# Attention scores lowered by their row maximum before the transpose, the exponential taken on the way out of PSUM

## The chip, the cores and the metric

The kernel runs on one core of a Trainium2 chip. The metric is the device time of one execution in microseconds (us); lower is better.

## The reference

One transformer block on x of 8 x 512 tokens x 256 features, all in float32. Attention comes first, then a mixture of experts:

```python
h = layernorm(x) * (1 + ca) + sa
q, k, v = split(h @ W_qkv + b_qkv)                      # 16 heads of 16
scores = q @ k.T / 4 + bias[h, i - j]                   # 512 x 512 for each of 8 x 16 heads
attn = softmax(scores, axis=-1)
x = x + ga * ((attn @ v) @ W_out + b_out)
h = layernorm(x) * (1 + cb) + sb
x = x + gb * (layernorm(sum of the 2 best of 8 experts) + h)
```

An expert is w_down(gelu(w_up(h))) with 1024 inner units. The change lies in the softmax of the attention alone.

## The kernel before, in words

The kernel has four stages: `prepare` (layer norm, the gates), `attention`, `route` (which token goes to which expert) and `experts`. Each engine runs a program of its own, written out by hand in the order in which it shall be done, and semaphores hold them together. There is no planner.

In `attention`, an outer loop runs over the 8 batches and an inner one over the 16 heads n (0 to 15) of a batch. The inner loop is written out. Batch 0 ("first") and batch 7 ("last") are written out too, and batches 1 to 6 ("middle") are one loop of the program (`Fori` in `by_batches`, L402), which every engine turns for itself. A head's scores are a 512 x 512 matrix, in four tiles t of 128 rows x 512 columns. For each head the engines do this:

- TensorE (`score`, L883) multiplies a tile of queries by the keys into one of two banks `ps_s`. The bank of tile t is free when VectorE has read tile t - 2 (`biased`).
- VectorE (`add_bias`, L753) adds the bias from the table `s_tile`, writes the negated sum into `sn` and takes its minimum over the row, the negated row maximum, into `mn`. It waits until the exponential has read that tile of `sn` for the head before (`exped`).
- ScalarE (`exp`, L680) writes exp(mn - sn) into `pr`, one tile of 128x512 at a time, four a head.
- TensorE (`turn_probabilities`, L891) transposes the 16 blocks of 128x128 of `pr` into the four banks `ps_t`, in two halves ("pairs") of eight.
- VectorE (`evacuate`, L764) copies the first half of `ps_t` (128x1024) into `pt`, ScalarE (`evacuate`, L685) the second half.
- TensorE (`weigh`, L900) multiplies `v`, which has a column of ones for the row sums, by `pt` into `ps_o`.

The heads overlap: in its stretch for head n TensorE does the scores of n, the transposes of n - 1 and the weighing of n - 2. The order is L1001 to L1017: scores 0 and 1, the shared use of n, transposes (first half), score 2, transposes (second half), score 3, weighing of n - 2. The shared uses (`USES`, L306) are the small works of the batch before and after, all through one bank `ps_m`: the projections q0, k0, q1, k1, v0, v1 of the next batch (at heads 1, 2, 9, 10, 12, 13), the transposes of results back0 to back3, turn0, turn1, rows0, rows1, the output projections out0 and out1 (heads 6 and 8), and the gate's logits (15.5, that is after head 15). ScalarE and VectorE read `ps_m` in the same order and free it (`used`, `freed`).

VectorE also has `moments` (after head 9), `centre` (L814, after head 10) and `normal` (L822, after head 12), of the batch before. GpSimd has work beside the heads, in an order of its own (`batch`, L631): it splits queries and keys into three bf16 parts (`split`, L409), splits a quarter of an expert's weights into two (`split_piece`, L571), adds the residual (`residual`, `add_x`), does `deviation` and `rest_of` for the layer norm, and moves v into place (`move_v`, L563). SP (`batch`, L504) issues the DMAs: loads of x and of weight pieces, stores of the parts and pieces after `split_done` and `w_low`, and reloads of the parts as stacks `qs` and `ks` for the next batch after head 7 and after head 15.

## Time and profile before

| | us |
|---|---|
| median of 3 runs | 1393.21 (1391.31 to 1395.48) |
| the profiled execution | 1397.81 |
| its span | 1396.2 |
| TensorE busy | 1152.0 (83%) |
| VectorE busy | 927.5 (66%) |
| ScalarE busy | 676.1 (48%) |
| GpSimd busy | 709.6 (51%) |
| the exponential, L683, ScalarE | 340.8, 512 instructions |
| the add of the bias, L761, VectorE | 332.3, 512 instructions |
| the transposes, L897, TensorE | 280.3, 2048 matmuls |
| the copy of the first half, L769, VectorE | 156.4, 128 instructions |
| the copy of the second half, L690, ScalarE | 131.2, 128 instructions |

The profile names engines PE (TensorE; PEld is its weight load), DVE (VectorE), ACT (ScalarE), POOL (GpSimd) and SP (the DMA issuer). In a row of the timeline stand start, duration, engine, line, operation, tile written and tiles read, shapes, count, and in brackets the idle time before it and who ended it. Matmuls are pipelined: a row's duration runs to the end of the last one, and the next can begin before it. A span of the profile is some 1.6 us less than the execution's own time.

### The profile page before, as it was taken

To read this page: it belongs to the slowest core of one execution; us is meant where nothing else is said; L and a number is where in the kernel's file an instruction comes from. 1 tells how busy PE (TensorE), PEld (TensorE's weight loads), DVE (VectorE), ACT (ScalarE), POOL (GpSimd) and SP (SyncE) were. 2 spreads that over 40 slices of the span, in tenths; PEclk is the share of its full clock that TensorE was granted. 3 is DMA by queue.
4 is the path that set the end of the run, shared out by engine and by line. 5 is a ranking of instruction groups with operands and counts; after the bars stand their busy time and mean duration, and the time that the engine had idled before them with its cause. 6 is when DMAs were issued, how large, how long until landed. Compare 5 with 4: busy or idle time off the path is not lost. (4 is left out here: it accounts for less than half of the span.)

```text
span 1396.2 us, 33418 instructions
## 1 busy us (share of the span) xinstructions
PE 1152.0 (83%) x11298; PEld 900.9 (65%) x11299; DVE 927.5 (66%) x2197; ACT 676.1 (48%) x1044; POOL 709.6 (51%) x726
## 2 busy tenths in 40 slices
PE   5569999898998998988999861399999999999900
PEld 3236776676766765766677541188888888888800
DVE  4548788587786885885888836655555555555566
ACT  4247776575765765765677620222222222222312
POOL 3215155343551553454423322866776777676756
PEclk9779999898998998998999975599999999999955
DMA  9597952663556346526644117124243344242364
GB/s 308 180 194 193 255 158 79 150 129 99 152 111 156 110 101 144 123 84 144 120 98 142 61 46 268 34 48 106 45 105 80 72 111 108 50 106 45 45 159 127
DMA packets 123679, 169.23 MB, mean 121 GB/s; under 512 B 13176, under 2 KB 99704, under 8 KB 123552
## 3 DMA queue, kind: packets, MB, share of 16 engines
q1 hardware_dynamic: 103136, 137.59, 37.3%
q0 software_dynamic: 20416, 29.94, 11.2%
q8 instruction: 80, 1.31, 0.4%
q14 instruction: 47, 0.39, 0.1%
HBM read 106.26 MB, written 61.23 MB: 120 GB/s over the span
## 5 line engine op out<-in xcount | busy, mean ns | idle before, releaser
L683 ACT ACTIVATE b_pr<-b_sn,b_mn 128x512 f32<-128x512 f32 x512 | 340.8, 714 | 133.1 <-DVE b_mn L761 128.8
L761 DVE CUSTOM_DVE_ANT_0 b_sn<-b_ps_s,s_tile 128x512 f32<-128x512 f32 x512 | 332.3, 685 | 91.0 <-PE b_ps_s L888 36.1
L897 PE MATMUL b_ps_t<-b_ident,b_pr 128*128 128x128 f32 x2048 | 280.3, 282 | 8.5 <-ACT b_pr L683 7.4
L897 PEld LDWEIGHTS b_ps_t<-b_ident,b_pr 128*128 128x128 f32 x2048 | 246.0, 146 | 54.2 <-ACT b_pr L683 21.2
L888 PE MATMUL b_ps_s<-b_ks,b_qs 96*128 96x512 bf16 x512 | 195.2, 403 | 58.7 <-DVE b_mn L761 31.6
L1594 PE MATMUL d_ps_u<-d_xp,k_wu 128*128 128x256 bf16 x1776 | 201.6, 274 | 0.0
L1609 PE MATMUL d_ps_y<-k_wd,d_gp 128*128 128x256 bf16 x1776 | 199.9, 273 | 0.0
L769 DVE COPY b_pt<-b_ps_t 128x1024 f32<-128x1024 f32 x128 | 156.4, 1222 | 54.9 <-PE b_ps_t L897 50.9
L1594 PEld LDWEIGHTS d_ps_u<-d_xp,k_wu 128*128 128x128 bf16 x1776 | 173.6, 98 | 21.7 <-issue 0.8
L1609 PEld LDWEIGHTS d_ps_y<-k_wd,d_gp 128*128 128x128 bf16 x1776 | 173.7, 98 | 20.2
L690 ACT ACTIVATE b_pt<-b_ps_t 128x1024 f32<-128x1024 f32 x128 | 131.2, 1025 | 108.5 <-PE b_ps_t L897 107.9
L1484 ACT ACTIVATE d_g<-d_ps_u 128x512 f32<-128x512 f32 x160 | 94.8, 598 | 129.4 <-PE d_ps_u L1594 128.9
L1437 POOL DMA_INDIRECT sums<-d_yo,d_places x80 | 133.2, 1665 | 41.6 <-issue 24.9
L912 PE MATMUL b_ps_o<-b_pt,b_v 128*32 128x128 f32 x4096 | 144.6, 284 | 0.2 <-ACT b_pt L690 0.2
L1520 DVE CAST d_xp<-d_ps_x 128x512 bf16<-128x512 f32 x41 | 28.3, 691 | 169.3 <-PE d_ps_x L1581 169.3
L912 PEld LDWEIGHTS b_ps_o<-b_pt,b_v 128*32 128x32 f32 x4096 | 108.3, 113 | 43.9 <-issue 42.6
L1493 ACT ACTIVATE d_yo<-d_ps_y,d_gates 128x256 f32<-128x256 f32 x80 | 33.5, 470 | 198.6 <-PE d_ps_y L1609 176.4
L888 PEld LDWEIGHTS b_ps_s<-b_ks,b_qs 96*128 96x128 bf16 x512 | 49.2, 98 | 114.9 <-DVE b_mn L761 71.8
L1533 DVE TENSOR_TENSOR d_gp<-d_g,d_gp 128x512 bf16<-128x512 f32 x160 | 110.8, 693 | 5.5
L1414 POOL DMA_INDIRECT d_xg<-h_rows,d_tokens x84 | 88.2, 1050 | 49.4 <-POOL d_tokens L1410 36.4
L1426 POOL DMA_INDIRECT d_gates<-gate_rows,d_places x80 | 77.2, 965 | 44.4 <-POOL d_places L1422 31.7
L1531 DVE CAST d_gp<-d_g 128x512 bf16<-128x512 f32 x160 | 74.4, 465 | 35.6 <-ACT d_g L1484 29.8
(192 smaller groups left out, 1244.7 us busy)
## 6 DMA issues: line engine op xcount, KB each, us to landing
w_parts<-b_w_split SPq DMA_DIRECT2D x32, 512.0 KB, 3.4
splits<-b_parts SPq DMA_DIRECT2D x32, 384.0 KB, 2.6
b_qs<-splits SPq DMA_DIRECT2D x96, 128.0 KB, 4.9
b_ks<-splits SPq DMA_DIRECT2D x96, 128.0 KB, 7.2
b_w_raw<-in_w_up_t SPq DMA_DIRECT2D x16, 512.0 KB, 8.9
b_w_raw<-in_w_down_t SPq DMA_DIRECT2D x16, 512.0 KB, 5.7
k_wu<-w_parts SPq DMA_DIRECT2D x8, 1024.0 KB, 4.9
k_wd<-w_parts SPq DMA_DIRECT2D x8, 1024.0 KB, 7.3
```

The lines of the kernel that those rows point to most:

```text
L683: act.activation(pr[:, m, t, :], sn[:, t, :], ACT.Exp, bias=mn[:, m, t:t + 1], scale=-1.0).then_inc(exped, 1)
L690: act.activation(pt[:, m, 2:4, :], ps_t[:, 2:4, :], ACT.Copy).then_inc(out_act, 1)
L761: dve.tensor_tensor_reduce(sn[:, t, :], ps_s[:, t % 2, :], ahead.tile[:, n, at:at + S], -1.0, BIG, ALU.add, ALU.min, mn[:, n % 2, t:t + 1] ...
L769: dve.tensor_copy(pt[:, m, 0:2, :], ps_t[:, 0:2, :]).then_inc(out_dve, 1)
L888: pe.matmul(ps_s[:, t % 2, :], qs[:, half, m, t * P:(t + 1) * P], ks[:, half, m, :], start=True, stop=True).then_inc(scored, 1)
L897: mm = pe.transpose(ps_t[:, j, t * P:(t + 1) * P], pr[:, m, t, j * P:(j + 1) * P], ident[:, :])
L912: mm = pe.matmul(ps_o[2 * DK * t:2 * DK * (t + 1), n % TB * P:(n % TB + 1) * P], v[:, j, n, :], pt[:, n % 2, j, t * P:(t + 1) * P], start= ...
L1437: pool.indirect_dma_start(sums, bass.IndirectOffsetOnAxis(ap=places[:, u, 0, i:i + 1], axis=0), yo[:, u, i, :], None, compute_op=ALU.add). ...
L1484: act.activation(g[:, j, :], ps_u[:, j, :], ACT.Gelu).then_inc(gelued, 1)
L1533: dve.tensor_tensor(gp[:, u, 1, at], g[:, j, :], gp[:, u, 0, at], ALU.subtract).then_inc(g_split, 1)
L1594: mm = pe.matmul(ps_u[:, j // 2, j % 2 * ROWS:(j % 2 + 1) * ROWS], kept.wu[:, slot, w, c, j * P:(j + 1) * P], xp[:, u, x, c * ROWS:(c + 1) ...
L1609: mm = pe.matmul(ps_y[:, i, 0:D], gp[:, u, x, j * ROWS + i * P:j * ROWS + (i + 1) * P], kept.wd[:, slot, w, j, :], start=(j == 0 and n == ...
```

## The change

The negated biased scores of a head now stay in `sn` as two buffers (one for even and one for odd heads), and `pr` is gone. Taking the maximum off is a step of its own, in place: GpSimd does tiles 0, 1 and 2 of a head (`lower`: multiply by -1, add the column of `mn`), ScalarE tile 3. TensorE transposes these lowered scores (`turn_scores`). ScalarE alone reads `ps_t`, both halves of 128x1024, and its exponential writes `pt`. VectorE has no evacuation left.

In TensorE's order the weighing of n - 2 comes behind scores 0 and 1 of head n, then the shared use, score 2, the first half of the transposes, score 3, the second half. VectorE's add waits for the transposes of the head before the last (`turned`).

GpSimd's side work is cut into pieces and placed between its `lower`s (`beside`, by head and half head): `split` becomes `split_high` and `split_low`, `split_piece` becomes `piece_high` and `piece_low`, and `residual` and `rest_of` are done in halves, the residual's add as two instructions of 128x512 in place of four of 128x256. The places are: move_v(1) at 0.5; splits 0 and 1 at heads 2 and 3, each high part before the first `lower` and low part between the second and third; residual at 4; pieces 0 and 1 at 5 and 6; add_x at 7 and 9; splits 2 and 3 at 10 and 11; deviation at 11.5; pieces 2 and 3 at 12 and 13; rest_of at 14 and 14.5; move_v(0) at 15.

```diff
@@ -338,9 +338,8 @@
         ks = sb("ks", [KS, 2, HALF, S], BF16)
         v_next = sb("v_next", [P, TB, D])
         v = sb("v", [P, TB, NH, 2 * DK])
-        sn = sb("sn", [P, TB, S])
+        sn = sb("sn", [P, 2, TB, S])
         mn = sb("mn", [P, 2, TB])
-        pr = sb("pr", [P, 2, TB, S])
         pt = sb("pt", [P, 2, TB, S])
         ot = sb("ot", [P, S])
         inv = sb("inv", [P, TB, TB])
...
+            def split_high(k, done, reads):
+
+                pool.wait_ge(freed, reads)
+                at_least(pool, parts_out[k % 2], (done - k % 2) * 8)
+                apart(pool, pool_passed)
+                pool.tensor_copy(parts[:, k % 2, 0, :], qf[:, k % 2, :]).then_inc(split_step, 1)
+                pool.wait_ge(split_step, done * 3 + 1)
+                pool.tensor_tensor(rest[:, :], qf[:, k % 2, :], parts[:, k % 2, 0, :], ALU.subtract).then_inc(split_step, 1)
+
+            def split_low(k, done):
+
+                pool.wait_ge(split_step, done * 3 + 2)
+                apart(pool, pool_passed)
+                pool.tensor_copy(parts[:, k % 2, 1, :], rest[:, :]).then_inc(split_step, 1)
+                pool.wait_ge(split_step, done * 3 + 3)
+                pool.tensor_tensor(parts[:, k % 2, 2, :], rest[:, :], parts[:, k % 2, 1, :], ALU.subtract).then_inc(split_done, 1)
+
...
+            def lower(b, n, t):
+
+                k = (b * NH + n) * TB + t
+                pool.wait_ge(biased, k + 1)
+                apart(pool, pool_passed)
+                pool.tensor_scalar(sn[:, n % 2, t, :], sn[:, n % 2, t, :], -1.0, mn[:, n % 2, t:t + 1], ALU.mult, ALU.add
+                                   ).then_inc(lower_pool, 1)
...
+            def beside(b, n, kind):
+
+                first, last = kind == "first", kind == "last"
+                if n == 0 and kind == "middle":
+                    load_h1(b + 1, uses_before(b, kind) - 1)
+                if n == 0.5 and not first:
+                    move_v(b, 1, uses_before(b, kind) - 1)
+                if n == 2 and not last:
+                    split_high(0, (b + 1) * 4, use(b, kind, "q0") + 1)
+                if n == 2.5 and not last:
+                    split_low(0, (b + 1) * 4)
...
+                for n in range(NH):
+                    beside(b, n, kind)
+                    lower(b, n, 0)
+                    lower(b, n, 1)
+                    beside(b, n + 0.5, kind)
+                    lower(b, n, 2)
...
@@ -677,17 +739,19 @@
                                ACT.Identity, bias=b_col[:, c:c + 1],
                                scale=(DK ** -0.5 if name[0] == "q" else 1.0)).then_inc(freed, 1)
 
-            def exp(h, m, t):
-
-                act.wait_ge(biased, h * TB + t + 1)
-                act.activation(pr[:, m, t, :], sn[:, t, :], ACT.Exp, bias=mn[:, m, t:t + 1], scale=-1.0).then_inc(exped, 1)
-
-            def evacuate(h, m):
-
-                act.wait_ge(turned, h * 2 + 2)
+            def lower(b, n):
+
+                t = TB - 1
+                act.wait_ge(biased, (b * NH + n) * TB + t + 1)
+                act.activation(sn[:, n % 2, t, :], sn[:, n % 2, t, :], ACT.Identity, bias=mn[:, n % 2, t:t + 1], scale=-1.0
+                               ).then_inc(lower_act, 1)
+
+            def exp(h, m, pair):
+
+                act.wait_ge(turned, h * 2 + pair + 1)
 
                 at_least(act, weighed, h - 1)
-                act.activation(pt[:, m, 2:4, :], ps_t[:, 2:4, :], ACT.Copy).then_inc(out_act, 1)
+                act.activation(pt[:, m, 2 * pair:2 * pair + 2, :], ps_t[:, 2 * pair:2 * pair + 2, :], ACT.Exp).then_inc(exped, 1)
 
             def turn_out(c, at):
 
...
@@ -715,14 +779,11 @@
                 for n in range(NH):
                     h = b * NH + n
 
-                    at_least(act, turned, (h - 1) * 2)
-                    exp(h, n % 2, 0)
-                    exp(h, n % 2, 1)
                     read_shared(b, n, kind)
                     if kind != "first" or n > 0:
-                        evacuate(h - 1, (n + 1) % 2)
-                    exp(h, n % 2, 2)
-                    exp(h, n % 2, 3)
+                        exp(h - 1, (n + 1) % 2, 0)
+                        exp(h - 1, (n + 1) % 2, 1)
+                    lower(b, n)
                     if n == 1 and kind != "first":
 
                         outputs(b * GROUPS - 1, uses_before(b, kind))
...
@@ -755,18 +817,11 @@
                 k = (b * NH + n) * TB + t
                 dve.wait_ge(scored, k + 1)
 
-                at_least(dve, exped, k - TB + 1)
+                at_least(dve, turned, (b * NH + n - 1) * 2)
                 apart(dve, dve_passed)
                 at = (TB - 1 - t) * P
-                dve.tensor_tensor_reduce(sn[:, t, :], ps_s[:, t % 2, :], ahead.tile[:, n, at:at + S], -1.0, BIG, ALU.add, ALU.min,
+                dve.tensor_tensor_reduce(sn[:, n % 2, t, :], ps_s[:, t % 2, :], ahead.tile[:, n, at:at + S], -1.0, BIG, ALU.add, ALU.min,
                                          mn[:, n % 2, t:t + 1]).then_inc(biased, 1)
-
-            def evacuate(h, m):
-
-                dve.wait_ge(turned, h * 2 + 1)
-
-                at_least(dve, weighed, h - 1)
-                dve.tensor_copy(pt[:, m, 0:2, :], ps_t[:, 0:2, :]).then_inc(out_dve, 1)
 
...
-            def turn_probabilities(h, m, pair):
-
-
-                at_least(pe, out_act if pair else out_dve, h)
-                for j in (2 * pair, 2 * pair + 1):
-                    for t in range(TB):
-                        mm = pe.transpose(ps_t[:, j, t * P:(t + 1) * P], pr[:, m, t, j * P:(j + 1) * P], ident[:, :])
+            def turn_scores(h, m, pair):
+
+
+                at_least(pe, exped, (h - 1) * 2 + pair + 1)
+                for t in range(TB):
+                    if pair == 0:
+                        if t < TB - 1:
+                            pe.wait_ge(lower_pool, h * (TB - 1) + t + 1)
+                        else:
+                            pe.wait_ge(lower_act, h + 1)
+                    for j in (2 * pair, 2 * pair + 1):
+                        mm = pe.transpose(ps_t[:, j, t * P:(t + 1) * P], sn[:, m, t, j * P:(j + 1) * P], ident[:, :])
                 mm.then_inc(turned, 1)
 
             def weigh(b, n):
 
                 h = b * NH + n
-                pe.wait_ge(out_dve, h + 1)
-                pe.wait_ge(out_act, h + 1)
+                pe.wait_ge(exped, h * 2 + 2)
...
                         pe.wait_ge(stack_in[n // HALF], (b + 1) * 32 * len(Q_PART))
                     score(b, n, 0)
                     score(b, n, 1)
-                    shared(b, n, kind)
-                    if kind != "first" or n > 0:
-
-                        pe.wait_ge(exped, h * TB)
-                        turn_probabilities(h - 1, (n + 1) % 2, 0)
-                        score(b, n, 2)
-                        turn_probabilities(h - 1, (n + 1) % 2, 1)
-                    else:
-                        score(b, n, 2)
-                    score(b, n, 3)
                     if n > 1:
                         weigh(b, n - 2)
                     elif kind != "first":
                         weigh(b - 1, n + NH - 2)
+                    shared(b, n, kind)
+                    score(b, n, 2)
+                    if kind != "first" or n > 0:
+                        turn_scores(h - 1, (n + 1) % 2, 0)
+                    score(b, n, 3)
+                    if kind != "first" or n > 0:
+                        turn_scores(h - 1, (n + 1) % 2, 1)
                     shared(b, n + 0.5, kind)
 
             by_batches(pe, batch)
-            pe.wait_ge(exped, B * NH * TB)
             for pair in range(2):
-                turn_probabilities(B * NH - 1, 1, pair)
+                turn_scores(B * NH - 1, 1, pair)
             weigh(B - 1, NH - 2)
             weigh(B - 1, NH - 1)
             back(B * GROUPS - 1, end_use("back3"))
```

## Rows read from the trace of the kernel before

**Rows 1.** Windows, core 0: busy us (instructions) by engine, TensorE's clock, DMA share, GB/s

```profile
core 0: us, PE busy (x) PEld busy (x) DVE busy (x) ACT busy (x) POOL busy (x), PEclk, DMA share, GB/s
...
264.94:359.68 94.74, 87.47 (x929) 64.76 (x928) 71.76 (x174) 63.48 (x92) 41.43 (x40) 0.93 0.53 122
...
90.00:825.00 735.00, 671.41 (x7347) 498.11 (x7346) 562.85 (x1352) 500.22 (x723) 305.72 (x292) 0.95 0.53 130
```

**Rows 2.** Timeline of ScalarE: L690 at head 1 of batches, and the last

```profile
90.95 1.02 ACT L690 ACTIVATE b_pt<-b_ps_t 128x1024 f32<-128x1024 f32 x1 [1.78 <-PE b_ps_t L897]
...
169.69 1.02 ACT L690 ACTIVATE b_pt<-b_ps_t 128x1024 f32<-128x1024 f32 x1 [1.19 <-PE b_ps_t L897]
...
645.81 1.03 ACT L690 ACTIVATE b_pt<-b_ps_t 128x1024 f32<-128x1024 f32 x1 [1.19 <-PE b_ps_t L897]
...
731.75 1.02 ACT L690 ACTIVATE b_pt<-b_ps_t 128x1024 f32<-128x1024 f32 x1 [0.78 <-PE b_ps_t L897]
...
810.78 1.02 ACT L690 ACTIVATE b_pt<-b_ps_t 128x1024 f32<-128x1024 f32 x1 [2.67 <-PE b_ps_t L897]
```

**Rows 3.** Timeline of one head of batch 5, 566.4 to 571.2 us

```profile
566.46 1.32 ACT L683 ACTIVATE b_pr<-b_sn,b_mn 128x512 f32<-128x512 f32 x2
...
566.66 0.67 PE L888 MATMUL b_ps_s<-b_ks,b_qs 96*128 96x512 bf16 x2
...
567.17 0.60 PE L943 MATMUL b_ps_m<-b_flip,b_on 128*128 128x128 f32 x4
...
567.84 1.09 PE L897 MATMUL b_ps_t<-b_ident,b_pr 128*128 128x128 f32 x8
...
568.77 0.38 PE L888 MATMUL b_ps_s<-b_ks,b_qs 96*128 96x512 bf16 x1
...
568.99 1.04 PE L897 MATMUL b_ps_t<-b_ident,b_pr 128*128 128x128 f32 x8
...
570.06 1.02 ACT L690 ACTIVATE b_pt<-b_ps_t 128x1024 f32<-128x1024 f32 x1 [0.18 <-PE b_ps_t L897]
...
570.17 1.08 PE L912 MATMUL b_ps_o<-b_pt,b_v 128*32 128x128 f32 x32
...
571.18 0.39 PE L888 MATMUL b_ps_s<-b_ks,b_qs 96*128 96x512 bf16 x1
```

**Rows 4.** Timeline, the turn of the loop from batch 1 to batch 2

```profile
245.96 1.02 ACT L690 ACTIVATE b_pt<-b_ps_t 128x1024 f32<-128x1024 f32 x1 [1.10 <-PE b_ps_t L897]
...
249.18 0.19 DVE L833 COPY logits<-b_ps_m 128x32 f32 x1 [1.88 <-PE b_ps_m L966]
...
253.26 1.92 PE L897 MATMUL b_ps_t<-b_ident,b_pr 128*128 128x128 f32 x8
...
255.84 0.69 DVE L761 CUSTOM_DVE_ANT_0 b_sn<-b_ps_s,s_tile 128x512 f32<-128x512 f32 x1 [6.46 <-issue]
...
264.94 1.02 ACT L690 ACTIVATE b_pt<-b_ps_t 128x1024 f32<-128x1024 f32 x1 [1.02 <-PE b_ps_t L897]
```

**Rows 5.** Timeline of TensorE, a head with a projection, batch 0

```profile
92.58 1.88 PE L929 MATMUL b_ps_m<-s_h,s_wqkv 128*128 128x512 f32 x4
94.30 0.93 PE L897 MATMUL b_ps_t<-b_ident,b_pr 128*128 128x128 f32 x7
```

**Rows 6.** By source line, L568, L618, L1175 (from 890.8 us), L819, L828: ns min/median/max

```profile
L568 POOL COPY b_v<-b_v_next x16: 604/609/620, 71.2 to 747.6; 128x512 f32<-128x512 f32 x16
...
L618 POOL TENSOR_SCALAR b_rstd<-b_mv x8: 227/228/496, 214.0 to 831.0; 128x4 f32<-128x4 f32 x8
...
L1175 POOL TENSOR_SCALAR c_hot_rest<-c_nums,c_place_f x7: 595/597/614, 890.8 to 894.3; 128x128 bf16<-128x128 f32 x7
...
L819 DVE SCALAR_TENSOR_TENSOR b_xb<-b_gated,b_mv,b_mod x32: 472/826/2335, 217.5 to 832.1; 128x256 f32<-128x256 f32 x32
...
L828 DVE SCALAR_TENSOR_TENSOR b_xb<-b_xb,b_rstd,b_mod x32: 473/478/484, 231.6 to 834.1; 128x256 f32<-128x256 f32 x32
```

**Rows 7.** Groups of GpSimd's instructions, 264.94 to 359.68 us

```profile
L419 POOL TENSOR_TENSOR b_rest<-b_qf,b_parts 128x512 f32<-128x512 f32 x4 | 4.7, 1174 | 0.3
```

More of the change, by code:

```diff
@@ L407, in by_batches, with split @@
             batch(B - 1, "last")
-        def split(engine, k, done, reads, passed=None):
+        def split(engine, k, done, reads):
             engine.wait_ge(freed, reads)
@@ L414, in split @@
             out = parts[:, k % 2, :, :]
-            if passed is not None:
-                apart(engine, passed)
             engine.tensor_copy(out[:, 0, :], qf[:, k % 2, :]).then_inc(split_step, 1)
@@ L659, in _ @@
+            def batch(b, kind):
+                for n in range(NH):
[4 more added lines that the diff above has]
+                    lower(b, n, 2)
             by_batches(pool, batch)
-            residual(B - 1)
+            for j in range(2):
+                residual(B - 1, j)
             for j in range(2):
@@ L663, in _ @@
             deviation(B - 1)
-            rest_of(B - 1)
+            for j in range(2):
+                rest_of(B - 1, j)
         @block.scalar
@@ L737, in _ @@
             by_batches(act, batch)
-            evacuate(B * NH - 1, 1)
+            for pair in range(2):
+                exp(B * NH - 1, 1, pair)
             outputs(B * GROUPS - 1, uses_before(B - 1, "last") + len(uses_of("last")))
@@ L871, in _ @@
             by_batches(dve, batch)
-            evacuate(B * NH - 1, 1)
             back(B - 1, 3, end_use("back3"))
```

119 lines of the change are left out of this document (68 added, 51 removed).

## The prediction, made before the change was run

> **What bounds the kernel now.** I read the windows first. The attention stage runs from about 90 to 825 us, 735 of the 1396 us, and TensorE is busy for 671 of them [rows 1]; every line that the change touches is in this stage, so the rest of the kernel is taken as unchanged. Next came ScalarE's timeline. One instruction, the evacuation at L690, occurs once a head, so its starts mark the heads: the 16 heads of batch 0 take 78.7 us, batches 1 to 5 take 95.2 us each (476.1 for five), batch 6 takes 85.9 and the 15 heads left take 79.0 [rows 2]. Then one head in the timeline [rows 3]. From its first score matmul (566.66) to the next head's (571.18) there are 4.52 us, and TensorE works nearly all through: two scores to 567.17, a shared use of 0.6 us, eight transposes every 0.93 us (567.84 to 568.77), 0.22 us for a score (568.77 to 568.99), 1.18 for the second eight and the last score, 1.01 for the weighing (570.17 to 571.18). Its waits are short. The reader should see why: every instruction waits for something of an earlier half head. The weighing in particular uses a head whose evacuation ended long before. Without the 0.6 us the work is 0.51 + 0.93 + 0.22 + 1.18 + 1.01 = 3.85 us a head. Last, the turn of the loop [rows 4]: VectorE stands 6.5 us with the releaser "issue" (249.4 to 255.8), and so it goes at the end of each of batches 1 to 5; heads 0 and 1 together take 19.0 us there (245.96 to 264.94). The change keeps the loop, so it keeps this stall.
>
> **What the change moves.** VectorE loses a copy of 128x1024 (1.22 us a head) and ScalarE has two PSUM exponentials of 128x1024 and one pass of 128x512 in place of four exponentials and a copy, 2.8 us a head for 3.9. Both were already under the 4.5 us of a head, so this gains only where they stop TensorE: heads 2 to 15 take 95.2 - 19.0 = 76.2 us, and TensorE's own work in them is 14 x 3.85 + 16.8 for shared uses (below) = 70.7, so there are 5.5 us a batch to be had, some of them where VectorE does moments and centre (L806 to L820) between two adds. TensorE has the same matmuls. What decides is their order and their waits.
>
> **The ring.** Before, the exponential came ahead of the transposes, and weighing head n-2 stood at the end of head n. Now the exponential comes behind the transposes, and weighing n-2 stands behind the first two scores of head n. But the second half of the transposes of n-2 is the last thing in head n-1. So only two scores (about 0.5 us) lie between the transposes and a weighing that waits for the exponential of their result. Everything else of TensorE lies behind that weighing, in the same order, and leads to the next head's transposes. It is a closed ring:
> - from the start of the second eight transposes to ScalarE's start on them: 570.06 - 568.99 = 1.07;
> - the exponential of 128x1024 from PSUM: no row has it; the copy of the same tile and size takes 1.02 to 1.03, taken as 1.03 (lower end: the same, as the engine reads and writes the same elements; two exponentials of 128x512 take 1.32, the upper end);
> - ScalarE's end to TensorE's start: 566.46 + 1.32 = 567.78, and the transposes behind it begin at 567.84: 0.05;
> - weighing 1.01, a score 0.22, eight transposes 0.93, a score 0.22.
> All from [rows 3]. The sum is 4.53 us a head plus any shared use, because shared uses stand inside the ring. TensorE idles about 0.7 us in each head. A head with no shared use took about 4.5 before and stays so; one with a 0.6 us use went for the same 4.5 and becomes 5.1; one with a projection (1.72 us, 92.58 to 94.30 [rows 5]) took 5.6 and becomes 6.25.
>
> **The sum.** Batches 1 to 5, heads 2 to 15: 14 x 4.53 = 63.4; five projections 8.6; two output projections, of about 1.7, 3.4; seven uses of 0.6, 4.2 (the eighth, 0.6 more of work, is at 14.5 and stands in the idle 0.7); and 1.5 for VectorE's centre at head 11: four instructions of 0.83 us at the median [rows 6] ahead of that head's first add, of which the ring's own wait covers about half; the ends are 0 and 4. That is 81.1. At the turn of the loop two things change: the logits no longer stand behind a score and a weighing, so VectorE's stall begins 1.3 us sooner; and eight transposes, which were done inside the stall (253.26, 1.92 us at half clock [rows 4]), now come after it, behind the third score. I take 20.3 for heads 0 and 1, which took 19.0. Batch: 101.4 against 95.2, +6.2, five times +31. Batch 6 without the stall: 81.1 + 5.7 + 4.5 = 91.4 against 85.9, +5.5. Batch 0: 16 x 4.53 + 6 x 1.72 + 3 x 0.6 = 84.6 against 78.7, +5.9. Batch 7: 68.0 for its heads, 3.4, 4.2, 2 at head 11 and 1.2 for the logits, 78.8 against 79.0: nothing. The last head's exponential before the last weighing: +1. Together +43.
>
> **GpSimd.** It gets 48 passes of 128x512 f32 a batch, each with a column from memory and two operations. No row has this form. Below stands the copy of that size, 0.61; above, a line through the two TENSOR_SCALARs of the trace, 0.228 for 4 columns and 0.597 for 128 with little beside it, which is 3.0 ns a column and 1.74 us for 512 [rows 6]. I take 0.70: like the copy it reads and writes one f32 tile, while the 128 columns belong to a comparison that writes bf16. The whole side work of a batch was 41.4 us busy [rows 1]; with 48 x 0.70 = 34 and some 0.1 us between 88 instructions it is 84 of 101, room on the whole. Locally it isn't even: a head with a split is 2 x 0.61 + 2 x 1.17 [rows 7] + 2.1 + 0.7 for gaps = 6.4 us against 5.1 at head 3. The third pass of a head is ready about 1.1 us after its third score and wanted a head later, so some 4 us of lag are covered; the splits and pieces of heads 2 to 6 use 2 to 3 of it. Heads 11 to 14 (two splits, pieces, two products of 128x512) touch the limit: 0.5 a batch, +4. SP's stores wait for the same splits as before, each now due half a batch or more before its stack is loaded; nothing there is near.
> The 128x512 pass is the one cost on which a page speaks with a figure. The Trainium skill's "GPSIMD Engine Reference" (section on elementwise, side-by-side cycle accounting) gives 769 ns for 512 elements in a good loop; the sum would then be higher by about 3 us, and no run so far has this form.
> The trace also shows an interference: the centre's instruction (two SBUF inputs) takes 472 to 2335 ns [rows 6], while its twin L828, for which GpSimd mostly stands idle, takes 473 to 484. With GpSimd busier, all four could take 2.3, 9.3 us instead of four medians, 3.3: at most +6 in each of seven batches, +42; I take none of it, since VectorE has room there. The Trainium skill's "SBUF — State Buffer" (who interferes with whom) says that such a VectorE instruction contends with a GpSimd one that reads SBUF; the trace agrees, and by that rule the scores' add (one input from PSUM) would stay at its 0.68 us.
>
> **Time.** +43 +4 = +47. The profiled execution took 1397.8 us (span 1396.2), 4.6 over the median of the runs, so 1445 becomes 1440 us against 1393.2.
>
> **Rivals.**
> - *TensorE is bound by its work alone.* If the weighing found its exponential done, a head would cost 3.85 plus uses, and VectorE's lost copy would also remove its stops: heads 2 to 15 would take 70.7 + 1.5 = 72.2 where they took 76.2. That is -4 a batch, some -30: 1363. It decides if ScalarE's exponential ended within the 0.5 us of the two scores; 1.07 + 1.03 from the row speak against it. Chance 0.07.
> - *GpSimd is the bound.* Beyond 101 = 48 X + 41 + 9, X = 1.07 us, every head waits for it. At 1.07 its crowded heads exceed the cover by about 9 a batch: near 1515. At 1.74 a middle batch takes 134, the first and last some 117: 1040 for the 720 of now, near 1700. For it: two operations with a pointer may be slower than a copy. Against: the rows of one input. Chance 0.15.
> - *The losses and gains cancel*, if the ring is 0.35 us shorter than its sum (a faster exponential, transposes let go by parts): within 0.3%, 4 us, about what a measurement of this kernel can tell from no change. Chance 0.03.
> The forecast has 0.75. Its own bounds: the ring 0.15 shorter and no stop at head 11, -29: 1411; an exponential of 1.34 adds 0.31 to each of 128 heads, +40, or the interference +42, 1482; GpSimd up to 1.07, 1515. The range 1408 to 1515 leaves out most of the 0.10 below and about half of the second rival. Slower 0.90, within 0.03, faster 0.07.
>
> **What would show it.** Right: TensorE's weighing is preceded by an idle of about 0.7 us released by ScalarE's exponential in nearly every head; ScalarE's second exponential repeats every 4.5, 5.1 or 6.3 us; batches of about 101 us; GpSimd's pass near 0.7 us, and few waits of the transposes for it. Wrong: weighings that start right behind the scores; passes over 1 us with the transposes waiting for GpSimd; a stop at the loop's turn that grew by more than 2 us; times outside attention that moved.

## The result, and the profile of the changed kernel

The changed kernel takes 1480.85 us (median of 4 runs, 1476.11 to 1486.82) against 1394.35 us (4 runs, 1391.31 to 1401.67) before: ratio 1.0625, interval 1.0581 to 1.067. It is slower by 86 us. The profiled execution has a span of 1474.5 us, 78.3 more than the 1396.2 of before.

The page of the changed kernel: the busy time of each engine, and of its part 5 (line, engine, operation, tiles, shapes, count; busy us, mean ns; idle us before them and what ended most of it) the groups of the change:

```profile
PE 1151.9 (78%) x11298; PEld 897.2 (61%) x11299; DVE 796.4 (54%) x2069; ACT 562.2 (38%) x788; POOL 963.5 (65%) x1094
...
L823 DVE CUSTOM_DVE_ANT_0 b_sn<-b_ps_s,s_tile 128x512 f32<-128x512 f32 x512 | 341.3, 689 | 280.2 <-PE b_ps_s L940 275.3
L643 POOL TENSOR_SCALAR b_sn<-b_sn,b_mn 128x512 f32<-128x512 f32 x384 | 264.0, 695 | 194.8 <-DVE b_mn L823 194.1
L754 ACT ACTIVATE b_pt<-b_ps_t 128x1024 f32<-128x1024 f32 x256 | 262.1, 1024 | 298.7 <-PE b_ps_t L954 290.6
...
L968 PE MATMUL b_ps_o<-b_pt,b_v 128*32 128x128 f32 x4096 | 145.7, 285 | 101.1 <-ACT b_ot L765 53.9
```

TensorE is busy for as long as before (1152.0), VectorE for 131 us less, ScalarE for 114 less, GpSimd for 254 more. GpSimd's new pass costs 0.695 us, and the PSUM exponential of 128x1024 costs 1.024. GpSimd's idle before its pass ended with VectorE's maximum (194.1 of 194.8 us), so it was early and not late. TensorE's weighing stood idle for 101 us.

The attention stage shows where the time is. Windows of the changed kernel, a middle batch and the stage (to be read beside [rows 1]; 90 to 902 us answers to 90 to 825 there):

```profile
283.98:388.08 104.10, 85.72 (x929) 63.09 (x928) 56.23 (x158) 49.52 (x60) 72.78 (x86) 0.97 0.49 115
90.00:902.00 812.00, 668.50 (x7338) 494.83 (x7338) 433.52 (x1222) 389.91 (x471) 553.97 (x655) 0.96 0.47 118
```

TensorE's busy time in the stage (668.5 for 671.4) and its clock (0.96 for 0.95) are as before; the stage is 77 us longer. All of the loss is TensorE standing idle in this stage. By the starts of the first exponential of each head, batch 0 takes 92.4 us, batches 1 to 5 take 102.6, 104.1, 110.3, 104.7 and 106.9, batch 6 takes 96.2, and the 15 heads left 82.3: 799.5, where [rows 2] give 719.8.

Two heads of the changed kernel's timeline, to be read beside [rows 3]. The first exponential shown belongs to a head with a 0.6 us use:

```profile
620.33 2.12 ACT L754 ACTIVATE b_pt<-b_ps_t 128x1024 f32<-128x1024 f32 x2 [0.50 <-PE b_ps_t L954]
...
622.50 1.08 PE L968 MATMUL b_ps_o<-b_pt,b_v 128*32 128x128 f32 x32 [0.62 <-ACT b_pt L754]
...
623.51 0.66 PE L999 MATMUL b_ps_m<-b_flip,b_on 128*128 128x128 f32 x4
...
624.00 0.38 PE L940 MATMUL b_ps_s<-b_ks,b_qs 96*128 96x512 bf16 x1
...
624.22 1.04 PE L954 MATMUL b_ps_t<-b_ident,b_sn 128*128 128x128 f32 x8
...
625.30 2.12 ACT L754 ACTIVATE b_pt<-b_ps_t 128x1024 f32<-128x1024 f32 x2 [0.50 <-PE b_ps_t L954]
625.32 1.04 PE L954 MATMUL b_ps_t<-b_ident,b_sn 128*128 128x128 f32 x8
...
627.31 0.71 ACT L746 ACTIVATE b_sn<-b_sn,b_mn 128x512 f32<-128x512 f32 x1
...
627.92 0.59 ACT L765 ACTIVATE b_ot<-b_ps_o 128x512 f32<-128x512 f32 x1
...
628.56 1.08 PE L968 MATMUL b_ps_o<-b_pt,b_v 128*32 128x128 f32 x32 [1.72 <-ACT b_ot L765]
```

The ring closes as forecast: the exponentials end at 620.33 + 2.12 = 622.45, the weighing starts 0.05 later after an idle of 0.62, and the next pair of exponentials starts 4.97 us after this one. But the second weighing waits for another instruction of ScalarE. Its exponentials end at 627.42; then come the pass of tile 3 (L746) and the copy of the weighing's result of the last four heads, `b_ot` (L765), and only at 628.51, 1.09 us later, may TensorE overwrite `ps_o`. Four heads share one bank of `ps_o`, so this comes once in four heads. The waits of TensorE for ScalarE in the changed kernel (engine, tile and line, what released it: us, times, the longest):

```profile
PE b_ps_o L968 <- ACT b_ot L765: 53.9, 31, 1.8
...
PE b_ps_o L968 <- ACT b_pt L754: 46.2, 83, 0.7
```

An ordinary weighing waits 46.2 / 83 = 0.56 us, one behind `b_ot` 53.9 / 31 = 1.74. My sum has no such term.

### The profile page after: what moved, and what is told of

Read it like the earlier page. It is cut to its first block and busy times, and to the rows that moved or that the text cites. A ratio compares the mean times of both kernels' runs of the same rounds, so it can differ in the third digit from the quotient of the medians.

```text
span 1474.5 us, 33671 instructions
## 1 busy us (share of the span) xinstructions
PE 1151.9 (78%) x11298; PEld 897.2 (61%) x11299; DVE 796.4 (54%) x2069; ACT 562.2 (38%) x788; POOL 963.5 (65%) x1094
## 5 line engine op out<-in xcount | busy, mean ns | idle before, releaser
L823 DVE CUSTOM_DVE_ANT_0 b_sn<-b_ps_s,s_tile 128x512 f32<-128x512 f32 x512 | 341.3, 689 | 280.2 <-PE b_ps_s L940 275.3
L643 POOL TENSOR_SCALAR b_sn<-b_sn,b_mn 128x512 f32<-128x512 f32 x384 | 264.0, 695 | 194.8 <-DVE b_mn L823 194.1
L754 ACT ACTIVATE b_pt<-b_ps_t 128x1024 f32<-128x1024 f32 x256 | 262.1, 1024 | 298.7 <-PE b_ps_t L954 290.6
L954 PEld LDWEIGHTS b_ps_t<-b_ident,b_sn 128*128 128x128 f32 x2048 | 246.0, 144 | 50.9 <-issue 18.7
L954 PE MATMUL b_ps_t<-b_ident,b_sn 128*128 128x128 f32 x2048 | 273.2, 277 | 1.9 <-POOL b_sn L643 1.9
L940 PE MATMUL b_ps_s<-b_ks,b_qs 96*128 96x512 bf16 x512 | 189.4, 398 | 45.6 <-issue 24.8
L968 PE MATMUL b_ps_o<-b_pt,b_v 128*32 128x128 f32 x4096 | 145.7, 285 | 101.1 <-ACT b_ot L765 53.9
L746 ACT ACTIVATE b_sn<-b_sn,b_mn 128x512 f32<-128x512 f32 x128 | 91.2, 712 | 17.3 <-DVE b_mn L823 17.3
```

What stands on the lines that cost most here:

```text
L643: pool.tensor_scalar(sn[:, n % 2, t, :], sn[:, n % 2, t, :], -1.0, mn[:, n % 2, t:t + 1], ALU.mult, ALU.add).then_inc(lower_pool, 1)
L754: act.activation(pt[:, m, 2 * pair:2 * pair + 2, :], ps_t[:, 2 * pair:2 * pair + 2, :], ACT.Exp).then_inc(exped, 1)
L823: dve.tensor_tensor_reduce(sn[:, n % 2, t, :], ps_s[:, t % 2, :], ahead.tile[:, n, at:at + S], -1.0, BIG, ALU.add, ALU.min, mn[:, n % 2, t ...
L940: pe.matmul(ps_s[:, t % 2, :], qs[:, half, m, t * P:(t + 1) * P], ks[:, half, m, :], start=True, stop=True).then_inc(scored, 1)
L954: mm = pe.transpose(ps_t[:, j, t * P:(t + 1) * P], sn[:, m, t, j * P:(j + 1) * P], ident[:, :])
L968: mm = pe.matmul(ps_o[2 * DK * t:2 * DK * (t + 1), n % TB * P:(n % TB + 1) * P], v[:, j, n, :], pt[:, n % 2, j, t * P:(t + 1) * P], start= ...
```

## The experiments

The theory that the result suggests (A): the loss is the ring through ScalarE, and every fourth head it is longer by the copy. The rivals: GpSimd's new passes, or something else of the new order, cost it. All kernels are edits of the changed one, except one that edits the kernel before. They ran in three groups, each beside the kernel before, which took 1390.03 us in the group of the first four, 1395.03 in that of the next three and 1396.05 in that of the last two. A ratio is to the kernel before of its group, and two kernels of different groups are best compared by what each takes above it; the changed kernel takes 86.5 us more than its own (1394.35).

**The copy ahead of the exponentials.** ScalarE copies `b_ot` before it waits for the transposes.

```diff
+                    if n == 1 and kind != "first":
+                        outputs(b * GROUPS - 1, uses_before(b, kind))
+                    if n in (5, 9, 13):
...
                     read_shared(b, n, kind)
                     if kind != "first" or n > 0:
                         exp(h - 1, (n + 1) % 2, 0)
                         exp(h - 1, (n + 1) % 2, 1)
                     lower(b, n)
-                    if n == 1 and kind != "first":
-                        outputs(b * GROUPS - 1, uses_before(b, kind))
-                    if n in (5, 9, 13):
...
```

> The changed kernel with one thing moved: ScalarE's copy of the weighed outputs (b_ot, L765) stands before the two exponentials of heads 1, 5, 9, 13 instead of behind them and behind the pass of tile 3. Theory A (the copy of b_ot is a second member of the ring: the weighing of head 4, 8, 12, 16 may not overwrite ps_o before it, and it starts only 0.7 + 0.6 us after the exponential): the 32 weighings no longer wait for it, 1.2 to 1.3 us each, so 38 to 42 us less than the changed kernel, near 1441 us. Theory B (what exceeds the forecast is GpSimd holding the transposes or the turn of the loop): less than 10 us, 1470 or more.

Measured 1445.42 us (1443.55 to 1451.62) against 1390.03, ratio 1.0409 (1.0371 to 1.0446). It is 35.4 us below the changed kernel's median, but 31.1 by what each takes above the kernel before (55.4 for 86.5) and 30.5 by the spans (1444.0 for 1474.5); 32 copies x 1.10 would be 35.2. The heads of 7.4 us became 6.4 to 6.5, and no wait for `b_ot` is left among these waits of TensorE:

```profile
PEld b_ps_o L968 <- ACT b_pt L754: 84.4, 97, 1.2
PE b_ps_o L968 <- ACT b_pt L754: 68.3, 114, 0.9
```

By the matmul's rows TensorE's weighings waited for ScalarE 100.1 us before this edit (53.9 + 46.2) and 68.3 after it. The stage itself, by the starts of the exponentials, is 25.1 us shorter: in a middle batch the four copies gave back 3.9 us, but the last of heads 2 to 15 then takes 6.1 us where it took 5.1, as its transposes wait 0.82 us for a pass of GpSimd. TensorE's waits for GpSimd are 8.3 us in this run and were 1.9.

**The weighing at the end of the head again.** TensorE weighs n - 2 behind the second half of the transposes, as before the change; `move_v(1)` of GpSimd goes from 0.5 to 7.5, so that the two don't wait for each other.

```diff
                     score(b, n, 0)
                     score(b, n, 1)
-                    if n > 1:
-                        weigh(b, n - 2)
-                    elif kind != "first":
-                        weigh(b - 1, n + NH - 2)
                     shared(b, n, kind)
                     score(b, n, 2)
...
                         turn_scores(h - 1, (n + 1) % 2, 1)
+                    if n > 1:
+                        weigh(b, n - 2)
+                    elif kind != "first":
+                        weigh(b - 1, n + NH - 2)
                     shared(b, n + 0.5, kind)
```

> The changed kernel with the weighing of n - 2 put back at the end of head n, behind the second half of the transposes (GpSimd's move of v for the second half of the heads goes from head 0.5 to 7.5, or it would wait for a weighing that waits for it). Theory A (the ring through the exponential and the weighing is what costs, the division of work among the engines is sound): TensorE is bound by its own 3.85 us a head plus shared uses, 1360 to 1400 us, faster than the changed kernel by 80 us or more. Theory B (the passes of GpSimd and ScalarE ahead of the transposes are what costs): it stays above 1430 us.

Measured 1408.68 us (1407.65 to 1411.55), ratio 1.014 (1.0113 to 1.0168): 67 us less than the changed kernel with `move_v` at 7.5 (1476.08, the next run), less than the 80 that A had named, and 9 above the upper end of A's figure. No wait for an exponential stands among TensorE's first waits any more; the next one took over. Timeline of a head of it:

```profile
192.20 0.69 DVE L823 CUSTOM_DVE_ANT_0 b_sn<-b_ps_s,s_tile 128x512 f32<-128x512 f32 x1 [1.57 <-PE b_ps_s L940]
...
192.96 0.39 PE L940 MATMUL b_ps_s<-b_ks,b_qs 96*128 96x512 bf16 x1 [0.38 <-DVE b_mn L823]
```

The changed order has nothing between scores 0, 1 and score 2 but the shared use, and score 2 needs the bank of score 0, which VectorE frees: TensorE's scores wait 52.7 us in this run for VectorE's adds, 11.8 in the changed kernel. A head without a use takes 4.7 us, not 3.9. So the change moved a second cover: before, eight transposes stood there [rows 3].

**Only move_v later**, to have its share of that run apart: in `beside`, `n == 0.5` becomes `n == 7.5`.

> The changed kernel with GpSimd's move of v at head 7.5 instead of 0.5, where it waits up to 10 us for the weighing of head 15 of the batch before, with the passes of head 0 and 1 queued behind it. Theory A (this wait is covered, as the passes of head 0 are needed only after that weighing): within 8 us of the changed kernel. Theory B (it delays the first heads of each batch): 2 us or more in each of seven batches, 14 us or more less.

Measured 1476.08 us (1469.97 to 1481.79), ratio 1.0614 (1.0567 to 1.066), no different from the changed kernel. GpSimd's wait of 45 us for the weighing was idle time it had.

**The kernel before, with the weighing alone moved** behind scores 0 and 1.

```diff
                     score(b, n, 0)
                     score(b, n, 1)
+                    if n > 1:
+                        weigh(b, n - 2)
+                    elif kind != "first":
+                        weigh(b - 1, n + NH - 2)
                     shared(b, n, kind)
...
                     score(b, n, 3)
-                    if n > 1:
-                        weigh(b, n - 2)
-                    elif kind != "first":
-                        weigh(b - 1, n + NH - 2)
```

> The kernel before with one thing moved: the weighing of n - 2 stands behind scores 0 and 1 of head n, as in the change; everything else as it was. Theory A (the place of the weighing makes the ring): it waits for ScalarE's evacuation of the last transposes, ring 1.07 + 1.02 + 0.05 + 1.01 + 0.93 + 0.22 = 4.3 us plus the shared use, and four times a batch for the copy of b_ot behind two exponentials; 30 to 80 us slower than before, 1425 to 1475 us. Theory B (the place of the weighing does not matter, the exponential behind the transposes does): within 10 us of before.

Measured 1545.82 us (1541.84 to 1551.67), ratio 1.1112 (1.1079 to 1.1144). The move alone costs more in the old kernel than the whole change does in the new one; it is far above the range I had given. The waits name the reason:

```profile
PEld b_ps_s L888 <- DVE b_mn L761: 197.3, 246, 1.9
PE b_ps_s L888 <- DVE b_mn L761: 113.4, 239, 1.5
...
PE b_ps_o L912 <- ACT b_ot L701: 31.1, 31, 1.1
```

In the old kernel VectorE reads half of `ps_t`, ahead of the adds of scores 2 and 3. The weighing at the end of a head had been the cover for these adds; without it scores 0 and 1 of the next head wait for the two banks, 113.4 us where before they waited 31.6. With VectorE's evacuation gone, the changed kernel has 11.8 us of that wait. Of theory A only the copy of `b_ot` shows (31.1 us): no weighing of this run waits for the evacuation, since it starts late enough. So the early weighing is bad in both kernels, by different waits, and the change's division of work takes off much of what its order puts on.

**Tile 2 by ScalarE too**, on top of the early copy: GpSimd then does two passes of 128x512 a head and ScalarE two.

```diff
-                t = TB - 1
-                act.wait_ge(biased, (b * NH + n) * TB + t + 1)
-                act.activation(sn[:, n % 2, t, :], sn[:, n % 2, t, :], ACT.Identity, bias=mn[:, n % 2, t:t + 1], scale=-1.0
+                for t in (TB - 2, TB - 1):
+                    act.wait_ge(biased, (b * NH + n) * TB + t + 1)
+                    act.activation(sn[:, n % 2, t, :], sn[:, n % 2, t, :], ACT.Identity, bias=mn[:, n % 2, t:t + 1], scale=-1.0
```

> The kernel e1_ot_early (changed kernel with the early copy of b_ot, 1445 us) with tile 2 of every head lowered by ScalarE too, so GpSimd does 2 passes a head instead of 3 (16 x 0.7 = 11 us less of GpSimd's work a batch). Theory A (the ring is the bound, GpSimd's work lies beside it but for a head or two): within 8 us of e1, 1437 to 1453. Theory B (GpSimd's queue holds the transposes in its crowded heads): 2 us or more a batch less, 1430 or below.

Measured 1461.55 us (1459.96 to 1462.96), ratio 1.0484 (1.0452 to 1.0516), more than with the early copy alone, which neither theory had: by 16 us as it stands, 14 by the spans, 11 by what each takes above the kernel before. Heads 2 to 15 are faster by about 2 us a batch (80.7 for 82.3 in batch 1). The loss that the trace shows is at the turn of the loop: heads 0 and 1 take 25.0 us there in the mean of five for 19.8. With what the other heads win back, the stage is only 5 us longer; the other 9 us of the spans lie before its first exponential and behind its last, where the two kernels are the same. TensorE's waits with the releaser "issue" are longer; timeline of this run, then of the one with the early copy alone:

```profile
370.35 1.03 PE L939 MATMUL b_ps_s<-b_ks,b_qs 96*128 96x512 bf16 x2 [5.72 <-issue]
...
379.29 1.96 PE L953 MATMUL b_ps_t<-b_ident,b_sn 128*128 128x128 f32 x8 [4.12 <-issue]
```

```profile
368.88 0.60 PE L940 MATMUL b_ps_s<-b_ks,b_qs 96*128 96x512 bf16 x2 [2.68 <-issue]
...
375.07 0.38 PE L940 MATMUL b_ps_s<-b_ks,b_qs 96*128 96x512 bf16 x1 [1.79 <-issue]
```

What makes this stall longer isn't shown: TensorE's program is the same but for the semaphore that it waits on before it transposes tile 2. It stays open.

**TensorE's whole order as before**, with the change's division of work (GpSimd and ScalarE lower, ScalarE's exponential reads PSUM) and `move_v` at 7.5:

```diff
                     score(b, n, 1)
-                    if n > 1:
-                        weigh(b, n - 2)
-                    elif kind != "first":
-                        weigh(b - 1, n + NH - 2)
                     shared(b, n, kind)
-                    score(b, n, 2)
                     if kind != "first" or n > 0:
                         turn_scores(h - 1, (n + 1) % 2, 0)
-                    score(b, n, 3)
+                    score(b, n, 2)
                     if kind != "first" or n > 0:
                         turn_scores(h - 1, (n + 1) % 2, 1)
+                    score(b, n, 3)
+                    if n > 1:
+                        weigh(b, n - 2)
+                    elif kind != "first":
+                        weigh(b - 1, n + NH - 2)
```

> The changed division of work (GpSimd and ScalarE lower, the exponential reads PSUM) with TensorE's whole order as it was before: scores 0 and 1, shared use, transposes, score 2, transposes, score 3, weighing (and GpSimd's move of v at head 7.5, as in e2). Theory A (in e2 what was left over TensorE's own work was score 2 waiting 0.4 us a head for VectorE's add of tile 0, as the transposes no longer stood between scores 1 and 2): 0.4 us less in each of some 60 heads and more, 1365 to 1390, 20 us or more below e2 (1409) and level with before or faster. Theory B (the passes ahead of the transposes cost more when these come sooner): 1400 or above.

Measured 1437.22 us (1433.58 to 1450.64), ratio 1.0338 (1.028 to 1.0396). The quiet heads take 3.7 to 4.2 us, as A said, but the batches take 96 to 105, as B said: now GpSimd is late. One row of TensorE's timeline:

```profile
296.36 0.66 PE L954 MATMUL b_ps_t<-b_ident,b_sn 128*128 128x128 f32 x4 [0.94 <-POOL b_sn L643]
```

Such waits are 32.1 us in all (33 times); the changed kernel had 1.9. Its slow ring and its order had covered GpSimd.

**The same with tile 2 by ScalarE**, so that GpSimd has 32 passes a batch and not 48:

> e7 with tile 2 of every head lowered by ScalarE too. Theory A (with the ring gone TensorE is faster than GpSimd in the heads with splits and pieces, so GpSimd's queue is next): 10 to 20 us below e7. Theory B (GpSimd is covered there too, or ScalarE's second pass comes too late for the transposes): the same as e7 within 8 us, or slower.

Measured 1364.41 us (1359.24 to 1367.4), ratio 0.9775 (0.9736 to 0.9814): this beats both kernels, with its whole interval below 1. It is 73 us less than without the step, several times what I had expected: 16 passes x 0.692 = 11 us of GpSimd's work went from each batch. By the starts of the exponentials the stage is 66 us shorter, of which some 16 lie at the turns of the loop (heads 0 and 1 take 19.3 us there in the mean, for 22.5) and 50 in the other heads, about 6 a batch. The waits for GpSimd account for half of it: 1.6 us are left of 32.1. Most of the other half is TensorE's own busy time, as windows from the first exponential to the last show, without the step and then with it:

```profile
89.52:844.14 754.62, 661.33 (x7252) 497.78 (x7251) 438.47 (x1221) 402.45 (x468) 554.16 (x652) 0.93 0.50 126
```

```profile
90.33:778.62 688.29, 632.78 (x7252) 485.10 (x7251) 431.80 (x1221) 463.12 (x594) 465.62 (x524) 0.97 0.54 137
```

The same 7252 matmuls take 28.5 us less, at a mean granted clock of 0.97 for 0.93. A stop can cost more than its length: in the kernel without the step, eight transposes behind one of 2.27 us, for an add of VectorE, took 1.91 us, for 1.04 elsewhere, at a granted clock of 0.54 (330 to 333 us). Against the kernel before it is alike: from the first evacuation to the last that one has 719.83 us with 660.11 busy at 0.95, so 27 of the 31.5 us won are busy time and 4 are idle time. How much of the busy time is the clock, and how much short waits that a row of pipelined matmuls hides, isn't separated. Windows of this kernel, a middle batch and the stage:

```profile
262.63:354.64 92.01, 81.64 (x929) 62.80 (x928) 56.61 (x157) 59.04 (x77) 62.29 (x70) 0.96 0.50 119
90.00:792.00 702.00, 642.66 (x7350) 492.37 (x7349) 433.18 (x1224) 466.85 (x599) 470.10 (x529) 0.96 0.53 136
```

TensorE is busy for 642.66 of 702 us. In a middle batch one head, with VectorE's centre, takes 7.6 to 9.2 us where others of its kind take 5.5; there TensorE waits 2 us for an add:

```profile
401.54 2.52 DVE L873 SCALAR_TENSOR_TENSOR b_xb<-b_gated,b_mv,b_mod 128x256 f32<-128x256 f32 x3
...
404.73 0.39 PE L939 MATMUL b_ps_s<-b_ks,b_qs 96*128 96x512 bf16 x1 [1.98 <-DVE b_mn L822]
...
406.14 1.08 PE L967 MATMUL b_ps_o<-b_pt,b_v 128*32 128x128 f32 x32
```

This head took 7.6 us. In batch 1 the stop is as long, but the clock falls behind it (granted 0.59 from 219 to 223.2 us), and the head takes 9.2:

```profile
218.81 0.39 PE L939 MATMUL b_ps_s<-b_ks,b_qs 96*128 96x512 bf16 x1 [1.98 <-DVE b_mn L822]
...
220.64 1.94 PE L967 MATMUL b_ps_o<-b_pt,b_v 128*32 128x128 f32 x32
```

**The centre in two halves**, on top of that:

```diff
                 if kind != "first" and n == CENTRED:
-                    centre(b - 1)
+                    centre(b - 1, range(0, 2))
+                if kind != "first" and n == CENTRED + 1:
+                    centre(b - 1, range(2, TB))
```

> As e8_old_order_tile2, but VectorE subtracts the centre of four token tiles in two halves, two tiles behind head 10 and two behind head 11, instead of four together. Theory: in e8 head 12 takes 7.6 to 9.2 us where a head with the same shared use takes 5.5, because the score tiles of heads 12 and 13 are lowered by GpSimd and ScalarE only after VectorE's adds, and those stand behind the whole centre; with two halves each head's slack takes its part, so 2 to 3 us go in seven batches: 1345 to 1350. Rival: the stop at head 12 is the moments of the next batch and not the centre, or the halves only spread the same delay over two heads: within 8 us of e8's 1364.4.

Measured 1358.88 us (1352.56 to 1364.49), ratio 0.973 (0.9685 to 0.9775). The slow head fell to 5.9 to 6.1 us, so the centre was what stopped it, but the next head but one takes 5.7 us in every middle batch, where it took 4.2 in some and 5.6 in others, and heads 2 to 15 of a middle batch win some 1.5 us, not 2 to 3. The intervals of this and the last kernel overlap; the gain of 5.5 us (6.6 by what each takes above the kernel before) isn't told from none. The mechanism stands, its size was too high.

**The shared use ahead of the weighing**, on top of the early copy, to test the ring itself: if TensorE's idle time before the weighing is part of a closed ring, work put there costs less.

```diff
+                    shared(b, n, kind)
                     if n > 1:
                         weigh(b, n - 2)
                     elif kind != "first":
                         weigh(b - 1, n + NH - 2)
-                    shared(b, n, kind)
                     score(b, n, 2)
```

> As e1_ot_early (ScalarE copies the weighing's result before its exponentials), but TensorE does the shared use of a head (products, a projection) before the weighing and not behind the scores that follow it: scores 0 and 1, shared use, weighing, score 2, and so on. Ring theory (a head is transposes to exponential to weighing to score 2 and back, and TensorE is idle in the ring while the exponential runs): the shared use fills idle time of about 0.7 us that the ring has before the weighing, so heads with a 0.6 us use fall from 5.0 to about 4.5 and those with a projection from 6.3 to about 5.6, some 9 us a batch and 70 in all: 1370 to 1390. Rival: the time before the weighing is not idle enough, or score 2 and the evacuations behind it come later by as much, so that a head still pays its shared use in full: within 10 us of e1's 1445.4.

Measured 1420.0 us (1417.25 to 1425.34), ratio 1.0187 (1.0155 to 1.0219): 25 us less than with the early copy alone, or 31 by what each takes above the kernel before, between the two theories. The weighings' waits for the exponential fell from 68.3 us to 16.6. In the quiet heads the ring theory gives the numbers: heads with a 0.6 us use fell from 5.0 to 4.5, those with a projection from 6.3 to 5.5 or 5.6, and the first eight of heads 2 to 15 in batch 1 from 45.3 to 40.1 us. A weighing of this run has this idle left:

```profile
191.94 1.08 PE L968 MATMUL b_ps_o<-b_pt,b_v 128*32 128x128 f32 x32 [0.19 <-ACT b_pt L754]
```

The next six heads took 37.0 us and still take 36.7: what holds them isn't the ring alone. The longest wait there is in the head with VectorE's `centre`, which takes 3.66 us here for its four instructions; TensorE waits 2.09 us for the add behind it. The rows of batch 2 in this run:

```profile
321.79 3.66 DVE L874 SCALAR_TENSOR_TENSOR b_xb<-b_gated,b_mv,b_mod 128x256 f32<-128x256 f32 x4
...
326.11 0.57 PE L940 MATMUL b_ps_s<-b_ks,b_qs 96*128 96x512 bf16 x1 [2.09 <-DVE b_mn L823]
```

Three heads later VectorE's `normal` lies beside GpSimd's splitting of a piece, 3.26 us for its four instructions, with a shorter wait behind it (batch 1):

```profile
234.14 2.13 POOL L596 TENSOR_TENSOR b_w_split<-b_w_raw,b_w_split 128x1024 bf16<-128x1024 f32 x1
...
235.70 3.26 DVE L883 SCALAR_TENSOR_TENSOR b_xb<-b_xb,b_rstd,b_mod 128x256 f32<-128x256 f32 x4
...
239.62 0.39 PE L940 MATMUL b_ps_s<-b_ks,b_qs 96*128 96x512 bf16 x1 [0.61 <-DVE b_mn L823]
```

## Why the prediction was right, and where it was not

- **The mechanism was right and is shown.** The weighing alone at the other place gives back 67 of the 86 us, and filling the idle time before it gives back 25 to 31 of what the early copy left. Its sizes held: 4.5, 5.0 and 6.3 us for heads that I put at 4.53, 5.1 and 6.25; the exponential 1.024 for 1.03; the handover 0.05; the idle before the weighing 0.62 for "about 0.7".
- **The sum was too small: +47 for a measured +86.5 (78.3 by the spans).** The step that failed is the one that lists the ring's members: I took ScalarE as giving TensorE only the exponential there. The weighing also waits for `b_ot`, and I did not ask where ScalarE's other instructions would stand once the weighing waited for ScalarE at all. Its price was readable: the pass and the copy that follow the exponentials, which the changed kernel shows to be 1.09 us every fourth head. The run with the early copy measures the term at 31 us (25 within the stage, where GpSimd's lateness took some of it back). With it the sum would have been 1440 + 31 = 1471, for a measured 1480.85.
- **The range held partly by luck.** Its part above 1440 was made for a slower exponential, the interference and a GpSimd pass of up to 1.07 us. None of these came; the term that did come was in none of the bounds.
- **The loop's turn: the right size for the wrong reason.** I took 20.3 us for heads 0 and 1, for 19.0 before; the five turns take 17.6 to 23.6, 20.4 in the mean, and those of before 18.4 to 20.3, 19.3 in the mean. But VectorE's stall of 6.5 us [rows 4], which I said would stay, doesn't show any more: VectorE's idle time there is 3.25 us and ends with TensorE, whose score waits for "issue", and which then works slowly: a weighing takes 1.94 us where others take 1.08. Timeline of the changed kernel:

```profile
271.81 1.02 PE L940 MATMUL b_ps_s<-b_ks,b_qs 96*128 96x512 bf16 x2 [2.70 <-issue]
...
272.70 0.69 DVE L823 CUSTOM_DVE_ANT_0 b_sn<-b_ps_s,s_tile 128x512 f32<-128x512 f32 x1 [3.25 <-PE b_ps_s L940]
...
272.76 1.94 PE L968 MATMUL b_ps_o<-b_pt,b_v 128*32 128x128 f32 x32
...
277.49 0.38 PE L940 MATMUL b_ps_s<-b_ks,b_qs 96*128 96x512 bf16 x1 [1.30 <-issue]
```

- **GpSimd: 0.70 taken, 0.692 at the median.** The row below is the changed kernel's by line (ns min/median/max). The transposes waited for it 4.9 us by the weight load's rows and 1.9 by the matmul's, in the whole run, near the +4 taken; with the early copy these became 11.8 and 8.3. The Trainium skill's "GPSIMD Engine Reference" (side-by-side cycle accounting) gives 769 ns for 512 elements in a good loop; the measurement decides, and here it is 10% less.

```profile
L643 POOL TENSOR_SCALAR b_sn<-b_sn,b_mn x384: 682/692/869, 81.9 to 885.1; 128x512 f32<-128x512 f32 x192
```

- **The interference moved.** I had the centre at L819 at up to +42 us, and took none of it. The centre, now L874, has a median of 0.481 us, less than the 0.826 of [rows 6], and it is its twin, now L883, that has 0.908 where it had 0.478. What it cost the changed kernel wasn't measured; the runs that went nearer to TensorE's own work met it (2.52 us for three instructions of the centre, 3.66 for four). By the Trainium skill's "SBUF — State Buffer" (who interferes with whom) the scores' add, with one input from PSUM, is spared; it takes 0.691 for 0.685 at the median, and the trace agrees.
- **The rivals.** "TensorE bound by its work alone" was put at 1363 us with heads 2 to 15 at 72.2. It didn't come, because the weighing didn't find its exponential done. The kernel with TensorE's old order and GpSimd relieved makes that condition true, and takes 1364.4, with heads 2 to 15 of batch 1 at 72.4. "GpSimd is the bound" didn't come at 0.69 us a pass, but its mechanism did, in the kernel with the old order: once the ring no longer covered it, GpSimd's passes stopped the transposes. The threshold of 1.07 us a pass held for batches of 101 us only; at 92 it stands lower, and the crowded heads decide before the mean does.
- **Two slips.** ScalarE's work of a head before is 4 x 0.666 + 1.02 = 3.7 us, not 3.9. And no lower clock of TensorE behind a stop is in the sum. In batch 0, put at 84.6 us and measured at 92.4, two of the three stops for the copy were followed by the lower clock: granted 0.58 from 135.9 to 139.3 us and 0.55 from 162.5 to 166.3, while behind the first, as long, it stayed at 1.00 (112 to 114.5 us). The rows of the head that takes 9.1 us, with a projection of 3.37 us where others take 1.99:

```profile
134.64 1.34 PE L968 MATMUL b_ps_o<-b_pt,b_v 128*32 128x128 f32 x32 [1.81 <-ACT b_ot L765]
...
135.92 3.37 PE L985 MATMUL b_ps_m<-s_h,s_wqkv 128*128 128x512 f32 x4
```

- **What stays open.** The execution grew by 86.5 us by the medians and 78.3 by the profiled spans; the 8 between are the profiled runs' own places (before 3.5 above its median, after 4.7 below). With the early copy, batches 1 to 5 take 102.1 us in the mean, batch 6 93.5 and batch 7 78.6, near the 101.4, 91.4 and 78.8 of the sum, so little of it is missing there. Batch 0 still takes 91.6 us for 84.6: the stops for the copy are gone from it, but one of 2.25 us for a pass of GpSimd has come, again with slow matmuls behind it. Why a stop is followed by the lower clock in one place and not in another wasn't tested.

## What to carry to other kernels

When an edit puts a consumer nearer to its producer on another engine, write down the closed ring (last instruction to next start, engine by engine) and then list every semaphore the consumer waits on, each with what its engine now does ahead of the signal: the second wait of the same matmul cost about 30 us here. When a division of work is to be judged, keep the order of the bounding engine fixed; the change's division, with one more tile given to ScalarE, is 2.3% faster than before in the old order, and was 4.8% slower in the new order even with the early copy. A slow ring hides other engines' lateness, so after it is removed look at the next engine before giving up the idea. And count a stop of TensorE at more than its length where the clock falls behind it: of 66 us won by relieving GpSimd, 28.5 were TensorE's own busy time.

## What the runs showed of the hardware

A stall with the releaser "issue" at the turn of a program loop isn't a constant of an engine. VectorE's, 5.2 to 6.8 us at the five turns of the kernel before, doesn't show in the changed one. TensorE had one of 2.5 to 3.8 us at each turn of the kernel before, two in the changed kernel, of 2.6 to 2.8 and 1.3 to 3.6 us, and two of 4.3 to 5.7 and 2.6 to 4.2 us in the one with the early copy and tile 2 lowered by ScalarE, whose TensorE program is nearly the same. After the first of them in the changed kernel's turn from batch 1 to 2 TensorE works at the lower clock: granted 0.51 (the level of 1.2 GHz) from 271.8 to 274.9 us, after an idle of 2.7 us, and the weighing there takes 1.94 us for 1.08. After the second, of 1.3 us, it worked at the higher level (granted 1.00 from 277 to 279). Stops of 1.81 us in the changed kernel and of 1.98 us in the one with the old order and tile 2 by ScalarE were followed by either level. The cause of the stalls wasn't isolated. A second surprise was how much GpSimd's work counts once the ring no longer covers it: taking 11 us of it from each batch gave about 6 us in the heads away from the loop's turn, though GpSimd is then busy for only 62.29 of the 92.01 us of a batch.
